# Idle matrix products ahead of the projections and during the first group's maxima, in a one-core decoder layer

## What is computed

```python
x = x + attn(layernorm(x))
# attn: q, k, v = x@Wq+bq, x@Wk+bk, x@Wv+bv ; 16 heads of 16, 4 query heads share one key head
scores = jnp.einsum('bghnd,bhsd->bghns', q, k)
attn   = jax.nn.softmax(scores / SCALE, axis=-1)
out    = jnp.einsum('bghns,bhsd->bghnd', attn, v)
```

## Time and profile before

| what | us |
|---|---|
| median of 3 runs (1757.11, 1757.17, 1769.86) | 1757.17 |
| the profiled execution | 1762.47 |
| its span, first to last instruction | 1760.7 |
| PE busy in it | 1693.5 (96%) |
| DVE busy | 1381.2 (78%) |
| ACT busy | 1098.9 (62%) |
| POOL busy | 358.0 (20%) |
| mean granted TensorE clock | 0.973 |

### The profile page before, as it was taken

How to read it: one execution, slowest core, us unless ns; L and a number is a source line. 1 busy time by engine, 2 the same in 40 slices (tenths; PEclk the granted TensorE clock), 3 DMA queues, 4 the chain that set the end, 5 groups by cost and what they waited for, 6 DMA issues and landing times. The chain is left out here.

```text
span 1760.7 us, 35513 instructions
## 1 busy us (share of the span) xinstructions
PE 1693.5 (96%) x11894; PEld 1103.3 (63%) x11895; DVE 1381.2 (78%) x2621; ACT 1098.9 (62%) x2272; POOL 358.0 (20%) x433
## 2 busy tenths in 40 slices
PE   7899999999999999999899999997899999999998
PEld 3443333333333333356588999985788888888887
DVE  6679999999999999634788999874757666666663
ACT  5237888888888888842477777782235555455542
POOL 2000000000000000040042222220120555555540
PEclk9759999999999999999999999998999999999999
DMA  6600221111111111153302231115424333333335
GB/s 219 184 18 17 42 37 35 30 30 30 30 30 30 30 30 30 36 164 107 144 21 69 76 107 40 50 48 188 160 72 154 50 51 54 54 52 50 53 57 159
DMA packets 93594, 124.80 MB, mean 71 GB/s; under 512 B 19307, under 2 KB 72863, under 8 KB 92863
## 3 DMA queue, kind: packets, MB, share of 16 engines
q1 hardware_dynamic: 75696, 99.34, 20.0%
q0 software_dynamic: 13728, 18.88, 6.7%
q10 hardware_dynamic: 4047, 4.91, 0.9%
HBM read 71.25 MB, written 46.60 MB: 67 GB/s over the span
## 5 line engine op out<-in xcount | busy, mean ns | idle before, releaser
L506 DVE TENSOR_REDUCE half_max<-psA 128x1 f32<-128x512 f32 x1024 | 633.6, 684 | 20.1 <-PE psA L559 18.8
L538 ACT ACTIVATE PT<-psB 128x1024 f32<-128x1024 f32 x512 | 518.5, 1025 | 132.1 <-PE psB L569 131.9
L559 PE MATMUL psA<-KS,QS 48*128 48x512 f32 x1024 | 403.1, 473 | 3.9 <-PEq L104 2.0
L569 PE MATMUL psB<-QS,KS 50*128 50x512 f32 x1024 | 370.9, 460 | 0.2 <-ACT PT L538 0.2
L588 PE MATMUL psO<-PT,VG 128*32 128x256 f32 x4096 | 332.4, 397 | 4.5 <-ACT OU L528 0.5
L559 PEld LDWEIGHTS psA<-KS,QS 48*128 48x128 f32 x1024 | 165.4, 194 | 226.1 <-DVE half_max L506 167.9
L588 PEld LDWEIGHTS psO<-PT,VG 128*32 128x32 f32 x4096 | 82.5, 108 | 195.4 <-issue 119.8
L1784 PE MATMUL m_psY<-swd_high,m_hT 128*128 128x256 f32 x824 | 173.4, 293 | 16.2 <-DVE m_hT L1919 11.9
L1387 ACT ACTIVATE x_probs<-x_scores,x_neg_max 128x77 f32<-128x77 f32 x512 | 176.3, 359 | 8.7 <-DVE x_neg_max L1292 8.6
L569 PEld LDWEIGHTS psB<-QS,KS 50*128 50x128 f32 x1024 | 147.7, 189 | 13.1 <-ACT PT L538 10.5
L1784 PEld LDWEIGHTS m_psY<-swd_high,m_hT 128*128 128x128 f32 x824 | 135.5, 191 | 31.0 <-DVE m_hT L1919 17.8
(11 more groups left out here) (221 smaller groups left out, 2672.0 us busy)
## 6 DMA issues: line engine op xcount, KB each, us to landing
QS<-q_parts SPq DMA_DIRECT2D x96, 128.0 KB
q_parts<-part SPq DMA_DIRECT2D x16, 512.0 KB, 4.3
OT<-OU SPq DMA_DIRECT2D x16, 512.0 KB, 3.4
mx_kept<-cx_mx SPq DMA_DIRECT2D x8, 616.0 KB, 5.7
cx_mx<-mx_kept SPq DMA_DIRECT2D x4, 1232.0 KB, 7.9
KS<-k_parts SPq DMA_DIRECT2D x32, 128.0 KB
xf_rows<-XF SPq DMA_DIRECT2D x32, 128.0 KB, 1.7
acc<-X SPq DMA_DIRECT2D x32, 128.0 KB, 1.8
```

The lines of the kernel that those rows point to most:

```text
L506: dve.tensor_reduce(half_max[:, h * (TB // 2) + t % (TB // 2), n:n + 1], psA[:, bank_of(slot, 2 * v + r), :], axis=AX.X, op=ALU.max).then_ ...
L538: act.activation(PT[:, k % 4, 2 * a:2 * a + 2, :].rearrange("p h n -> p (h n)"), psB[:, u % 2, :, :].rearrange("p a n -> p (a n)"), ACT.Ex ...
L559: pe.matmul(psA[:, bank_of(slot, m), :], QS[top:top + KQ, slot, h // 2, t * P:(t + 1) * P], KS[top:top + KQ, slot, n * HALF:(n + 1) * HALF ...
L569: mm = pe.matmul(psB[:, u % 2, r, :], KS[top:top + KM, slot, c * P:(c + 1) * P], QS[top:top + KM, slot, a, half * HALF:(half + 1) * HALF], ...
```

## The change

Two places get products whose results nobody reads.

- In `phase_qkv`, PE waits for the constants first, issues 18 products of `ident` by `ident` (128x128 by 128 columns, float32) into the bank of `psQ` that the first projection overwrites later, and only then waits for the weights.
- In `phase_attention`, a function `keep_busy` issues three products of 128x128 by 512 columns (float32r, from `KS`) into `psO`, which the first group's values overwrite later. It is called once after each of the 26 pairs of the opening loop, 78 products in all. They wait for no semaphore and signal none.

```diff
+IDLE_PRODUCTS = 3
+FIRST_PRODUCTS = 18
@@ phase_qkv, PE
+            pe.wait_ge(consts, 3)
+            for n in range(FIRST_PRODUCTS):
+                pe.matmul(psQ[:, 0, 0:P], ident[:, :], ident[:, :], start=True, stop=True)
             pe.wait_ge(w_loaded, 16 * 5)
-            pe.wait_ge(consts, 3)
@@ phase_attention, PE
+            def keep_busy():
+
+                for n in range(IDLE_PRODUCTS):
+                    pe.matmul(psO[:, 0, :], KS[:, 0, 0:P], KS[:, 0, 0:HALF], start=True, stop=True)
+
             pe.wait_ge(loaded[0], NLOAD)
             for v in range(NC + LEAD):
                 for r in range(2):
                     pass_a(0, 0, v, r)
+                keep_busy()
```

## The result

The changed kernel takes 1770.95 us in the median of 20 executions (1757.03 to 1788.64), the kernel before 1756.43 us (20 executions, 1750.74 to 1769.86). The ratio is 1.0061, with a 95% interval from 1.0040 to 1.0083: slower, by less than 1%. This ratio leaves out the longest executions, over 1783 us, as disturbed ones; the experiments show that here they are the far end of the effect itself, and the medians are 0.8% apart.

A forecast was written before the change was run, and what follows sets the result against it. DVE was taken to pace the opening loop and slow PE only the units from u = 4. 1762.47 - 0.6 + 1.0 + 0.7 gave 1763.6 against the profiled execution, 1758 us at the median's; range 1746 to 1769.

The forecast's parts named there:

- rival C: Opening loop: idle products do not raise the clock, PE bounds it, 26 rounds cost 18 to 33 us; 1775 to 1790; chance 0.08.
- the low stretch behind u = 4: Group 0's units from u = 4 on, at the low clock: 2.16 us each, a stretch of about 29 us.
- B: Units u = 0 to 3 keep the clock, winning 11.0 us behind them: 1752 us, 1751 to 1756; chance 0.38.
- That DVE and not PE sets the pace of the loop: Opening loop of pass A: DVE busy 29.83 of 29.90 us, so a faster PE would buy nothing there.
- only the stretch behind u = 4 can be won: Group 0 from u = 4: DVE's idle time behind the slow PE, 11.0 us to win; nothing in u = 0 to 3.
- The thin units lose the clock (A): Group 0, u = 0 to 3, half-height scores without idle products: clock lost, later units 2.16 us; 1758 us; chance 0.50.
- its own sign of being wrong: Behind u = 4: the forecast is wrong if the low stretch is missing or much shorter than 29 us.
- The level in the loop: Opening loop: high clock throughout, or low for about two rounds costing 1.4 to 2.6 us; 0.7 taken at even odds.
- The cost at the high clock: Opening loop: three idle products a round cost 0 to 4.4 us in 26 rounds at the high clock; 1.0 taken.
- The first products: Kernel's opening: 18 products hidden behind DVE's normalising; second transposes gain 1.0 us at most; 0.6 us gain taken.

The follow-up runs named there:

- late6_fill: Changed kernel with idle products only in the loop's last three rounds, six each, and two in each unit u = 0 to 3, no bridge: 1752.76 us, ratio 0.9976.
- bridge2_fill: Changed kernel with two idle products a round, ten just ahead of the loop and two in each unit u = 0 to 3 of group 0: 1752.08 us, ratio 0.9971.
- after_again: The changed kernel run once more without any edit: 1769.08 us, ratio 1.0070 to the kernel before.
- bridge3: Changed kernel plus ten idle products (a bridge) in PE's wait just ahead of the loop, thin units not filled: 1757.37 us, ratio 1.0008.

## Why the prediction was right or wrong

It forecast no change by over 1%, at 1758 us with a range of 1746 to 1769. The ratio is within 1%, but the median of 1770.95 lies 2 us above the range, and thirteen of the 20 executions (1770 to 1789 us) lie where rival C was put, which had a chance of 0.08. That the ratio came out near no change is in part luck: the loop cost more than the sum had for it, and the low stretch behind u = 4 less. In the sums themselves, B's lower end comes to 1762.47 - 11.0 - 1.0 = 1750.5 and not 1751; nothing hangs on it.

- **That DVE and not PE sets the pace of the loop, and that only the stretch behind u = 4 can be won: right.** late6_fill shows it directly, a low clock in the loop at no cost. With the clock kept, the idle time ahead of the maxima fell by 10.6 us (bridge2_fill); the forecast was 11.0, from the same profile.
- **The thin units lose the clock (A): right in most of the profiles, wrong in the length.** Where the clock was high up to them and they were not filled, it fell at their end in three profiles (112.8 us in after_again, 113.0 in the loop products alone, 132.0 with six) and was kept in one (bridge3), so B happens too. Two rules of the Trainium skill ("TensorE: Matmul & The Clock Gate") stood against each other there: that of "A second HAM failure mode", by which short idles between groups of products make the clock swing, and that of the closing table. The first three profiles agree with the former, with pairs of scores that start 0.60 us apart; the profile of bridge3, with the same 0.60 us, does not. The forecast named its own sign of being wrong, a low stretch behind u = 4 missing or much shorter than 29 us. It is 13.6, 20.5 and 17.1 us long in the three profiles, 20 us in that of the change, and missing in bridge3: the units crawled at 2.16 us, as forecast, but not for as long.
- **The level in the loop: the step that failed.** "The idle products are of that kind, so I expect the loop to be at the high clock throughout, or low at its start for as long as there (66.1 - 62.7 = 3.4 us), about two rounds": this was priced at 0.7 us. In the profiled execution it was low for all 26 rounds, 28 us. The products were of the kind of the projections, the round as a whole was not: it changes twice between scores on 48 rows and products on 128 rows. Three idle products took 75.20 - 73.63 = 1.57 us to the next score in place of 3 x 0.43, and a pair of scores, side by side, 73.63 - 72.91 = 0.72 us in place of 0.43. The projections that I compared them with have no such changes. That these thinner rounds are why the clock stayed low is argued and not shown. For it: rounds with six products brought the clock back in two rounds, and at the loop's end in time for u = 4 (late6_fill). Against it: three products did so in two rounds in other executions. The low round of 2.29 us was inside the bounds given, 1.89 to 2.49; it was the number of such rounds that was wrong, 26 in place of 2.
- **C as all or nothing: wrong.** I gave it the condition that idle products do not raise the clock at all. They raise it in some executions after two rounds and in others not within the loop, and the time spreads over 31 us. The prediction had a time for half of the rounds (1766 to 1774), but no more than C's 0.08 for all of it.
- **The cost at the high clock: inside the bounds, above the value taken, and for another reason.** 1.33 us a round make 26 x 0.13 = 3.4 us; 1.0 was taken from 0 to 4.4. The upper bound stood for two scores one after the other. In the trace they go side by side, two in 0.50 us, and the round is long all the same:

```profile
77.83 0.50 PE L563 MATMUL psA<-KS,QS 48*128 48x512 f32 x2
78.26 0.98 PE L623 MATMUL psO<-KS 128*128 128x512 f32 x3
79.17 0.50 PE L563 MATMUL psA<-KS,QS 48*128 48x512 f32 x2
```

  From the scores to the first idle product it is 0.43 us, and from there to the next scores 0.91, where 0.23 and 0.69 were put.
- **The first products: hidden as forecast, and worth nothing that can be measured.** They end before the transposes, which are now short; in this execution the clock is kept:

```profile
1.61 6.60 PE L356 MATMUL psQ<-ident 128*128 128x128 f32 x36 [1.61 <-POOL ident L185]
9.81 0.67 PE L317 MATMUL psT<-ident,xn 128*128 128x128 f32 x4 [1.60 <-DVE xn L239]
...
14.35 0.76 PE L317 MATMUL psT<-ident,xn 128*128 128x128 f32 x4 [0.36 <-DVE xn L239]
```

The second transposes came at 14.35, 1.2 us earlier than in the earlier trace rows; 1.0 us was given as the most. In five of the ten profiles with first products the clock is kept like this; in the other five it falls again at 11.5 to 12.5 us, as the prediction had allowed for. That a gain reaches the end, the last step of the sum, was not seen in any pair of kernels.

## What to carry to other kernels

Idle products kept a clock that was already high in every profile with a bridge and filled units. As a means to raise it, three between the scores of a round did so in some executions only; six did so in the profiles that have them. At the low clock the three cost 1.57 us a round in place of 0.91, on the engine that the others then wait for. Find first where the low clock costs anything: here it was free while VectorE set the pace, so a few dense products just ahead of the costly stretch, and none in front of it, did as well as keeping the clock up throughout. And fill every thin stretch between the idle products and the work they are for, or the clock may be gone by then.

## What the runs showed of the hardware beyond that

- The same program spreads over 31 us (1757 to 1789), and its clock goes with it: the mean granted clock of the 20 executions goes from 0.988 at 1757.03 us down to 0.966 at 1788.64 us. One profile of such a kernel shows one of its cases, and the two profiles of the change here show different ones.
- A busy PE did not mean a high clock: PE is busy 59.85 of 59.85 us in the slow loop and 13.50 of 13.50 us in the units behind the thin ones, and the clock was 0.50 in both.
- A round that changes between products on 48 and on 128 rows takes longer than its parts. In the short profile a pair of scores starts every 1.33 us, where three idle products of 0.23 us and a pair side by side, taken at the same 0.23, make 0.92 us. Whether the change of height or the loading of new weights at it costs the 0.4 us, no run separates.
